# Moving the low-part subtractions of two weight units from VectorE to GpSimd, inside the feed-forward stage

## The reference, cut to what matters

```python
# first block's feed-forward layer
def act_quant(x):
    scale = 127.0 / jnp.clip(jnp.max(jnp.abs(x), axis=-1, keepdims=True), 1e-05)
    q = jnp.clip(jnp.round(x * scale), -128.0, 127.0) / scale
    return q
def bitlinear(x, w, b):
    xq = act_quant(rmsnorm(x)); wq = weight_quant(w)
    return jnp.einsum('bsd,fd->bsf', xq, wq) + b
h = bitlinear(x, w1, b1)          # 1024 -> 512
h = jax.nn.gelu(h, approximate=False)
out = bitlinear(h, w2, b2)        # 512 -> 1024
...
x = x + ffn(layernorm(x))
xn = layernorm(x)
...
x1 = xn @ W1 + b1                 # L1_gnn: 1024 -> 512; this is "g1"
alpha = jnp.tanh(x_i @ Wi + x_j @ Wj + bg[k])    # the gates, computed from x1 and its sums
```

## Time and profile before

| | us |
|---|---|
| median of 3 runs | 809.42 |
| lowest and highest run | 805.88, 810.45 |
| the profiled execution | 808.73 |
| span of its profile, first to last instruction | 807.0 |
| TensorE busy (share of the span) | 776.1 (96%) |
| VectorE busy | 588.6 (73%) |
| ScalarE busy | 385.1 (48%) |
| GpSimd busy | 49.9 (6%) |

### The profile page before, as it was taken

The page is one execution under the profiler, slowest core; times in us unless marked ns, Lnnn a source line. Parts: engine busy times, 40 slices in busy tenths (PEclk is TensorE's granted clock), DMA queues, the critical chain, the costliest instruction groups (busy, mean ns, idle before and its releaser), DMA issues. The chain is left out here.

```text
span 807.0 us, 11521 instructions
## 1 busy us (share of the span) xinstructions
PE 776.1 (96%) x4270; PEld 686.8 (85%) x4270; DVE 588.6 (73%) x1242; ACT 385.1 (48%) x798; POOL 49.9 (6%) x86
## 2 busy tenths in 40 slices
PE   5999999999999899999997699999999989999998
PEld 4888878889999899998875388888888879999886
DVE  8988878645555888997698958789896686675331
ACT  5222122454434667775657546575673323464220
POOL 3000000000000001001103211000002020000000
PEclk9999999999999999999999999999999999999999
DMA  5522123332334323239964439334135136444331
GB/s 191 183 77 79 53 78 132 130 130 80 131 108 147 98 73 114 76 113 300 262 251 83 127 89 265 102 104 158 53 105 144 56 111 154 131 131 147 127 132 39
DMA packets 28775, 102.17 MB, mean 127 GB/s; under 512 B 3736, under 2 KB 3864, under 8 KB 28464
## 3 DMA queue, kind: packets, MB, share of 16 engines
q1 hardware_dynamic: 24784, 86.76, 32.4%
q0 software_dynamic: 3936, 14.68, 8.2%
HBM read 91.99 MB, written 1.57 MB: 116 GB/s over the span
## 5 line engine op out<-in xcount | busy, mean ns | idle before, releaser
L1175 DVE TENSOR_TENSOR w_lo<-raw,w_hi 128x1024 fp32r<-128x1024 f32 x140 | 170.0, 1222 | 65.1 <-ACT w_hi L892 64.6
L892 ACT ACTIVATE w_hi<-raw 128x1024 fp32r<-128x1024 f32 x140 | 147.5, 1059 | 110.5 <-PE bank L1932 84.1
L1881 PE MATMUL bank<-xn1T,w_hi 128*128 128x384 f32 x448 | 115.2, 338 | 0.4 <-DVE xn1T L1166 0.4
L1932 PE MATMUL bank<-w_hi,xn3T 128*128 128x512 f32 x288 | 92.0, 393 | 0.0
L1881 PEld LDWEIGHTS bank<-xn1T,w_hi 128*128 128x128 f32 x448 | 79.9, 188 | 1.5 <-DVE w_lo L1175 0.8
L1881 PE MATMUL bank<-xn1T,w_lo 128*128 128x384 f32 x224 | 75.0, 335 | 0.0
L1881 PE MATMUL bank<-xn4T,w_hi 128*128 128x384 f32 x256 | 65.2, 335 | 0.4 <-DVE xn4T L1166 0.4
L1932 PEld LDWEIGHTS bank<-w_hi,xn3T 128*128 128x128 f32 x288 | 54.1, 188 | 11.1
L1932 PE MATMUL bank<-w_lo,xn3T 128*128 128x512 f32 x144 | 56.0, 389 | 0.0
L1881 PEld LDWEIGHTS bank<-xn4T,w_hi 128*128 128x128 f32 x256 | 46.1, 188 | 0.6 <-DVE w_lo L1175 0.6
L1881 PE MATMUL bank<-xn4T,w_lo 128*128 128x384 f32 x128 | 42.8, 335 | 0.0
(11 more groups left out here) (352 smaller groups left out, 1688.1 us busy)
## 6 DMA issues: line engine op xcount, KB each, us to landing
raw<-weights SPq DMA_DIRECT2D x140, 512.0 KB, 3.3
row_sb<-rows SPq DMA_DIRECT2D x6, 512.0 KB, 5.8
kcat<-kcat POOLq DMA_DIRECT2D x16, 192.0 KB, 3.0
base<-rows POOLq DMA_DIRECT2D x6, 512.0 KB, 14.1
w2r<-w_in SPq DMA_DIRECT2D x1, 2048.0 KB, 10.0
w1r<-w_in POOLq DMA_DIRECT2D x1, 2048.0 KB, 10.0
x_sb<-x_in SPq DMA_DIRECT2D x3, 512.0 KB, 4.7
row_sb<-rows SPq DMA_DIRECT2D x6, 256.0 KB, 4.8
```

The costliest lines, as they stand in the source:

```text
L892: act.activation(w_hi[:, u % RING], raw[:, u % RAW], ACT.Copy).then_inc(hi_split, 1)
L1175: dve.tensor_tensor(w_lo[:, u % RING], raw[:, u % RAW], f(w_hi[:, u % RING]), ALU.subtract).then_inc(unit_split, 1)
L1881: last = pe.matmul(out_of(pr)[:, 0:N], w[pa][:, slot, k * P:(k + 1) * P], TT[src][:, pb, k], start=(k == 0 and m == 0), stop=(k == KD - 1 ...
L1932: last = pe.matmul(out_of(pr)[:], tile[:, pa, k, ts], w[pb][:, at_, j * HALF:(j + 1) * HALF], start=(kk == 0 and j == 0 and m == 0 and nam ...
```

## The change

In `STEPS`, the two last `("ahead_lo",)` in front of g1 are taken out, and a new step `("pool_lo", i)` for i = 2 and 3 is put in earlier: the first behind `h_ev` 0 and `ahead_hi`, the second behind `square` 2. At it GpSimd waits until the unit before has been subtracted and ScalarE's copy of this one is there, then does the same subtraction of 128x1024 and increments `unit_split`. VectorE passes over these two units and, ahead of its next subtraction, waits once for GpSimd's second.

```diff
                   ("gelu", 1), ("square", 1), ("h_max", 1), ("h_T", 0), ("hn", 2), ("h_ev", 0), ("ahead_hi",), ("pool_lo", 2), ...
-                  ("h_round", 1), ("ffn_o", 0), ("square", 2), ("h_max", 2), ...
+                  ("h_round", 1), ("ffn_o", 0), ("square", 2), ("pool_lo", 3), ("h_max", 2), ...
-                  ("x_out", 1), ("x_norm", 0), ("xn3_T", 0), ("ahead_lo",), ("xn3_hi", 0), ("x_norm", 1),
-                  ("xn3_lo", 0), ("ahead_lo",), ("x_out", 2)])
+                  ("x_out", 1), ("x_norm", 0), ("xn3_T", 0), ("xn3_hi", 0), ("x_norm", 1),
+                  ("xn3_lo", 0), ("x_out", 2)])
...
+                if s[0] == "pool_lo":                                  # GpSimd
+                    u = UNIT_OF[("g1", s[1])]
+                    pool.wait_ge(unit_split, u)
+                    pool.wait_ge(hi_split, u + 1)
+                    pool.tensor_tensor(w_lo[:, u % RING], raw[:, u % RAW], f(w_hi[:, u % RING]),
+                                       ALU.subtract).then_inc(unit_split, 1)
...
             def split_unit(u):                                         # VectorE
                 dve.wait_ge(hi_split, u + 1)
+                if u == UNIT_OF[("g1", 3)] + 1:
+                    dve.wait_ge(unit_split, u)
...
+                if kind == "pool_lo":                                  # VectorE
+                    split[0] += 1
```

More of the change, by code:

```diff
@@ L176, in schedule @@
                   ("h_factor", 0), ("h_round", 0), ("ffn_h", 2), ("hn", 1), ("h_cast", 0), ("ahead_lo",),
-                  ("gelu", 1), ("square", 1), ("h_max", 1), ("h_T", 0), ("hn", 2), ("h_ev", 0), ("ahead_hi",), ("h_factor", 1), ("gelu", 2),
-                  ("h_round", 1), ("ffn_o", 0), ("square", 2), ("h_max", 2), ("h_cast", 1), ("h_factor", 2), ("h_round", 2),
+                  ("gelu", 1), ("square", 1), ("h_max", 1), ("h_T", 0), ("hn", 2), ("h_ev", 0), ("ahead_hi",), ("pool_lo", 2), ("h_factor", 1), ("gelu", 2),
+                  ("h_round", 1), ("ffn_o", 0), ("square", 2), ("pool_lo", 3), ("h_max", 2), ("h_cast", 1), ("h_factor", 2), ("h_round", 2),
                   ("h_T", 1), ("h_cast", 2), ("x_out", 0), ("h_ev", 1), ("h_T", 2), ("ffn_o", 1), ("h_ev", 2), ("ffn_o", 2),
-                  ("x_out", 1), ("x_norm", 0), ("xn3_T", 0), ("ahead_lo",), ("xn3_hi", 0), ("x_norm", 1),
-                  ("xn3_lo", 0), ("ahead_lo",), ("x_out", 2)])
+                  ("x_out", 1), ("x_norm", 0), ("xn3_T", 0), ("xn3_hi", 0), ("x_norm", 1),
+                  ("xn3_lo", 0), ("x_out", 2)])
     run("g1", 0, 4)
```

## The result

The change makes the kernel slower by 0.42%: ratio 1.0042, 95% interval 1.0030 to 1.0053, medians of 20 runs each 811.29 us against 807.89. Two of the twelve runs of e9 took 1314 us at a mean clock of 0.56, and its ratio is that of the other ten. The forecast was 811.5 us with +0.3%. The profiled execution of the changed kernel took 810.26 us, with a span of 808.5.

A forecast was written before the change was run, and what follows sets the result against it. TensorE was taken to bound the kernel, through its first g1 matmul. Stalls of 1.55 and 1.52 less a gain of 0.63 make +2.44 us: 811.2 or 811.9 by base, written as 811.5, range 808.0 to 815.0.

The forecast's parts named there:

- What bounds the stretch: TensorE, 96% busy, bounds the kernel; whatever moves the first g1 matmul from 459.67 us moves the end equally.
- The gain of 0.63: Without VectorE's subtraction of g1.2, the low parts of `xn3` 0 end at 458.89 instead of 459.52 us.
- T = 2.23 us: Time of one GpSimd subtraction of 128x1024, taken as two input reads; bounds 1.0 and 3.1 us.
- rival 3: Same stall at `h_round` with longer GpSimd subtractions: over 0.5% slower from 3.03 us each, 815 at 4 us; chance 15%.
- The stalls, 1.55 and 1.52: VectorE's `h_round` 1 and 2 each wait for a started GpSimd subtraction, by 1.55 and 1.52 us.
- rival 1: One stall only: `h_round` 2 goes ahead of the second GpSimd subtraction; +0.9 us, 810; chance 15%.
- rival 2: GpSimd's two-input subtraction leaves VectorE room at `h_round`, so no stall: 808.1 to 808.8 us; chance 15%.
- The sum of 2.44: Two `h_round` stalls less the gain at `xn3` 0: 1.55 + 1.52 - 0.63 = 2.44 us later.
- rival 4: Stalls plus TensorE's clock falling at `ffn_o` 1 and 2: up to +4.1 us, 812.9 to 813.6; chance 15%.
- move by about the same 3.1 us and end before the transposes: TensorE's `ffn_o` 1 and 2, 3.63 us for 16 matmuls, shift about 3.1 us and finish before the following transposes.
- A TensorE clock below 1 while `ffn_o` runs: A sign in the changed profile, at TensorE's `ffn_o` matmuls, that would show the forecast wrong; no size given.
- rival 5: GpSimd reaches its subtractions so late that TensorE waits for g1.2, wanted past 461 us; chance 2%.

The follow-up runs named there:

- e9: The change itself, measured once more on one chip beside two kernels with filled waits; ratio 1.0039 against the kernel before.
- e7: e4's kernel with 3, 5 and 6 unused filling matmuls in TensorE's waits; ratio 0.9978 against the kernel before.
- e6: The kernel before, with 3, 5 and 9 unused matmuls filling TensorE's idle time; ratio 0.9979 against the kernel before.
- e3: The change with GpSimd subtracting one column of each unit instead of 1024, queues and waits kept; ratio 0.9975 against the kernel before.
- e2: The kernel before, VectorE keeping its subtractions, plus two GpSimd subtractions of 128x1024 on unneeded data; ratio 1.0021 against the kernel before.
- e8: The change with each GpSimd subtraction cut into two of 128x512, the second issued after the first; ratio 1.0024 against the kernel before.
- e4: The change with its two GpSimd subtractions moved later, to run beside `x_out` 0 and 1; ratio 0.9981 against the kernel before.
- e5: The change, with 9, 12 and 6 unused matmuls filling TensorE's idle time; ratio 1.0019 against the kernel before.
- e1: The change's first part only: GpSimd subtracts g1.2, VectorE subtracts g1.3 at its old place; ratio 1.0015 against the kernel before.

## Why the prediction was right, step by step

- **What bounds the stretch**: right in that the end follows the first products of g1: their end is 1.55 us later, the span 1.5. But the prediction made it one number, the shift of the first g1 matmul, and said that the end moves by the same amount. That matmul moved by 3.12 us and the span by 1.5, because the matmuls behind it ran at the lower clock before and at the full clock now.
- **The gain of 0.63**: right in size. Between e7 and e6, which differ in it alone at a full clock, it is 0.65 us. In the change itself the low parts of `xn3` 0 end 0.84 us behind ScalarE's high parts (462.65 and 461.81), where 0.83 was forecast and 1.46 stood before.
- **T = 2.23 us**: 2.35 and 2.34, 5% more, far from the 3.1 us of a third pass for the float32r output (rival 3 is out). That the working came so near is in part luck. It started from 0.55 us for one element, a row of a power and not of a subtraction. A subtraction of one column took 0.19 us in e3, so the pace is (2.35 - 0.19) / 1023 = 2.11 ns an element, not 2 x 0.82 = 1.64. With 0.19 and 1.64 the forecast would have been 1.87 us. The estimate from the Trainium skill (GPSIMD Engine Reference, 3.1 Elementwise — side-by-side cycle accounting), 2.25 us, is as near as the forecast.
- **The stalls, 1.55 and 1.52**: measured 1.58 and 1.49 (2.07 and 1.98 less 0.49). The start of the second subtraction, 450.73 forecast, was 450.63, so rival 1 did not happen.
- **No stall at all (rival 2)**: out, by e2 and e3. The row that spoke for it, at 449.40, comes again in e3: a GpSimd power of 128x1 runs from 449.55 to 450.10, and the `h_round` instruction that starts at 449.89 keeps its 0.49 us. So a short GpSimd instruction did not hold up VectorE in two profiles, and the long one did. The Trainium skill's lock (SBUF — State Buffer, SBUF: two separate sides) agrees with e8, where the engines alternate instruction by instruction, and with e4, where VectorE's instructions with one SBUF tensor input beside a PSUM one pass.
- **The sum of 2.44**: at a full clock, 2.45 (e5 against e6).
- **The clock (rival 4, 15%)**: this was given too little. It is not an alternative to the forecast but comes with it: in every profile of an unfilled kernel with a stall (the change, e1, e2, e8, e9) TensorE is nearly idle for some microseconds, and the clock falls there. The step that failed is the one that let `ffn_o` 1 and 2 "move by about the same 3.1 us and end before the transposes": they took 5.24 and 6.25 us in the two profiles of the change (6.16 in e1's), not 3.63, and held up `x_out` 1 and the transposes. "A TensorE clock below 1 while `ffn_o` runs" was one of the prediction's own signs of being wrong, and it came true. Rival 4 put up to 1.7 us on top, "or less if the clock is then up when g1 begins", and this last is what both profiles of the change show. What neither the forecast nor the rival took off is the fall that the kernel before pays for in the same stretch (1.57 us), and which the change no longer has.
- **What is left open**: the two medians are 3.4 and 2.9 us apart from before, the stall at a full clock 2.45. The clock of the stretch does not explain the rest: with the waits filled in both kernels, e5 and e6 are still 3.0 us apart by the medians. The rest may be noise, as 2.44 us is 0.30%, the lower end of the first interval (1.0030 to 1.0053) and inside the second (1.0023 to 1.0056). These runs do not settle it.
- **The sign, the range and the time**: 0.42% slower, as forecast within 0.5%, and 811.29 in a range of 808 to 815. That 811.29 is so close to the 811.5 written down is luck. The forecast set 2.44 us on a base of 808.73 to 809.42, but the median of 20 runs of the kernel before is 807.89, 0.8 to 1.5 us lower. The measured step was larger by 1 us, and the two errors cancel.
- **Two slips that cost nothing**: g1.2 is wanted behind 12 matmuls of g1 and not six (so rival 5 had more cover still), and the chances of the forecast and the five rivals add up to 112%.

## What to carry to other kernels

An engine that is 6% busy is not free if it shares something with the busy one: look which forms of instruction are due on VectorE while GpSimd would run, and place the GpSimd work beside those that read a PSUM bank or make statistics. Moved there, the same two subtractions turned +0.4% into -0.2%. And where a stall leaves TensorE idle in a stretch of thin work, expect its clock to fall there, but subtract the fall that the kernel before already pays for in the same stretch: here 1.57 us went and 0.73 or 1.71 us came.

## What the runs showed of the hardware

- A GpSimd subtraction of 128x1024 float32 into float32r takes 2.35 us, of one column 0.19 us; VectorE's of 128x1024 takes 1.22 us. Two of 128x512 on GpSimd take 2.68 us with one of VectorE's instructions in between.
- A VectorE `tensor_scalar` on 128x512 float32, from SBUF to SBUF, does not run beside GpSimd's subtraction and ends 0.3 us behind it. VectorE's 128x1 instructions beside it kept their 0.15 and 0.17 us (450.89 and 451.08 in the changed kernel), and `x_out` and the statistics did not grow (e4). A GpSimd power of 128x1 did not hold up `h_round` (before, e3).
- Matmuls of no use kept the clock up in the stretch at no visible cost to the path: 12 bf16 matmuls in a wait of 3.07 us left 0.48 us of it, and in the kernel before the path kept its 11.90 us.
- The place where the clock falls is not fixed: at g1 in the profile of before, at `ffn_o` in those of e3 and e4, whose TensorE work ahead of it is the same.
- A fall of the clock costs what TensorE had to do in it: one fall of 1.7 us of full clock cost 1.57 us at g1 (before against e6) and 0.80 us at `ffn_o` (e4 against e7).
